# Small weights first in both load queues, all aggregation matmuls ahead of the first convolution, and one transpose for a unit's input where there were two

## The reference, cut to what matters

```python
# x (128, 64, 1024), cond (128, 128), all float32
x = x + conv1d(x, w0, pad=4, groups=4)            # w0 (64, 16, 9)
      + (cond @ cw.T)[:, :, None] + side[None, :, None]
h = gelu(cond @ W0 + b0);  h = gelu(h @ W1 + b1)
att = softmax(h @ W2 + b2)                        # (128, 8)
agg_w = einsum('bk,koi->boi', att, experts)       # one 64x64 matrix for each sample
x = x + einsum('boi,bih->boh', agg_w, x) + (att @ bias_k)[:, :, None]
```

## Time and profile before

| what | value |
|---|---|
| median of 3 runs | 252.88 us |
| the profiled execution | 252.83 us |
| its span, first to last instruction | 251.0 us |
| outside the span | 1.83 us |
| PE busy | 239.5 us, 95% |
| DVE busy | 223.1 us, 89% |
| ACT busy | 89.5 us, 36% |
| POOL busy | 27.1 us, 11% |
| moved by DMA | 68.72 MB, mean 274 GB/s |

### The profile page before, as it was taken

One profiled execution on the slowest core, in us unless ns is written; L12 is line 12 of the kernel. 1 busy time (PEld: TensorE's weight loads), 2 busy tenths in 40 slices (PEclk: granted clock), 3 DMA queues, 4 the chain that ended last, 5 costly groups with the idle time before them and its releaser, 6 DMA issues.

```text
span 251.0 us, 5804 instructions
## 1 busy us (share of the span) xinstructions
PE 239.5 (95%) x2180; PEld 95.4 (38%) x2180; DVE 223.1 (89%) x146; ACT 89.5 (36%) x144; POOL 27.1 (11%) x52
## 2 busy tenths in 40 slices
PE   7399999999999999999999999999999999999973
PEld 5263233333333333333333344344444444434531
DVE  0531899999999999999999999999999999999683
ACT  2305353321433333341505233333415052333453
POOL 1030422010101010010101010100101010101000
PEclk9659999999999999999999999999999999999999
DMA  6999693999999999999999999998989998444376
GB/s 145 262 306 274 136 200 60 334 231 407 329 375 240 381 240 339 293 319 305 272 350 238 387 228 373 276 361 249 335 292 287 342 262 347 167 167 168 123 293 256
DMA packets 29770, 68.72 MB, mean 274 GB/s; under 512 B 3312, under 2 KB 5616, under 8 KB 29760
## 3 DMA queue, kind: packets, MB, share of 16 engines
q1 hardware_dynamic: 19824, 51.41, 63.0%
q10 hardware_dynamic: 9936, 17.17, 26.2%
HBM read 35.02 MB, written 33.55 MB: 273 GB/s over the span
## 4 chain that ended last, share of the span: by engine, by line
PE 93%; DMA 2%; DVE 2%; SPq 1%; issue 0%; ACT 0%; DVEq 0%
PE yps L534 64%; PE zps L557 21%; DMA xin<-in_x 2%; PE yps L616 2%; PE yps L573 2%; PE zps L516 2%; DVE xph L414 1%; SPq L199 1%; DVE ynat L483 1%; PE zps L596 0%; PE yps L596 0%; PE zps L585 0%; PE zps L634 0%; DVE ycol L476 0%; ACT xin L380 0%
## 5 line engine op out<-in xcount | busy, mean ns | idle before, releaser
L534 PE MATMUL yps<-xph,wraw 64*64 64x512 f32 x1488 | 167.4, 591 | 0.0
L308 ACT ACTIVATE zout<-zps,gamu 128x512 f32<-128x512 f32 x120 | 72.9, 688 | 130.9 <-PE zps L557 87.9
L534 PEld LDWEIGHTS yps<-xph,wraw 64*64 64x64 f32 x1488 | 60.0, 132 | 100.2 <-issue 99.8
L422 DVE STREAM_TRANSPOSE ycol<-yps 128x1024 f32<-128x1024 f32 x62 | 74.5, 1220 | 9.2 <-PE yps L534 8.5
L414 DVE STREAM_TRANSPOSE xph<-xin 128x2112 f32<-128x2112 f32 x32 | 74.8, 2339 | 2.5 <-DMA xin<-in_x 2.5
L432 DVE STREAM_TRANSPOSE ynat<-ycol 128x2048 f32<-128x2048 f32 x30 | 67.6, 2291 | 1.1
L557 PE MATMUL zps<-ynat,mixv 64*64 64x512 f32 x480 | 57.6, 589 | 0.0
L244 POOL COPY mixv<-mixt 128x512 f32 (+1 forms) x16 | 17.5, 1094 | 178.9 <-ACT zout L308 174.5
L557 PEld LDWEIGHTS zps<-ynat,mixv 64*64 64x64 f32 x480 | 19.9, 132 | 30.3 <-issue 29.3
L316 ACT ACTIVATE mixt<-zps 128x1024 f32<-128x1024 f32 x8 | 7.8, 1021 | 17.3 <-PE zps L516 17.3
L616 PE MATMUL yps<-zout 128*128 128x256 f32 x20 | 8.9, 632 | 2.2 <-POOL zout L250 1.3
(11 more groups left out here) (54 smaller groups left out, 29.1 us busy)
## 6 DMA issues: line engine op xcount, KB each, us to landing
out<-zout SPq DMA_DIRECT2D x60, 512.0 KB, 5.3
xin<-in_x ACTq DMA_DIRECT2D x60, 258.0 KB, 7.5
xin<-in_x SPq DMA_DIRECT2D x60, 258.0 KB, 7.3
out<-xin SPq DMA_DIRECT2D x2, 512.0 KB, 3.2
out<-xin SPq DMA_DIRECT2D x4, 256.0 KB, 2.2
xin<-in_x ACTq DMA_DIRECT2D x4, 132.0 KB, 5.0
xin<-in_x SPq DMA_DIRECT2D x4, 130.0 KB, 5.0
xin<-in_x SPq DMA_DIRECT2D x4, 128.0 KB, 6.7
```

Of the source, the lines that this page charges most:

```text
L308: nc.scalar.activation(zout[:, o].rearrange("p (i c j q) -> p c i j q", i=2, c=2, q=PH)[:, c], zps[:, at:at + BANK].rearrange("p (q i j) - ...
L422: nc.vector.transpose(ycol[:, :, :, :, :, g].rearrange("p i s j q c -> p (i s j) q c"), yps[:, 2 * BANK * (g % 2):2 * BANK * (g % 2) + 2 * ...
L534: last = nc.tensor.matmul(yps[C * c:C * c + C, at:at + BANK].rearrange("p (s f) -> p s f", s=S // 2), wsum[rows, b, g], xph[slot][c][rows, ...
```

## The change

Seven edits are made together:

- SP issues `mlps`, `shares` and the experts `mixw` ahead of all of x; ACT issues `wraw` (the convolution weights) ahead of its part of x. `mixw` is 128 KB instead of 256 KB.
- `attt` is made by four ACT copies with a scale, where DVE made it in one instruction.
- The aggregation is two calls of 8 matmuls of 32 rows by 64 columns, where it was four calls of 4 matmuls of 32 rows by 128 columns; the even and odd channel blocks lie on the two partition halves of `mixt`. Four `gather` copies are left of eight.
- Both calls stand ahead of the first convolution, with `keep_on(3)` ahead of the transposed `att`, behind it, and between the calls; the `keep_on(6)` is gone.
- `mixv` is written by ACT in four copies of 64 partitions by 256 elements a unit, in the middle of the evacuation of the unit before, where POOL wrote it in one copy. POOL keeps `gamu`.
- A unit's x is turned in one transpose (4160 columns; unit 0 in two, of 2112 and 2048) and `ynat` is made in one (4096 columns).
- ACT's loads of unit 1 are issued in two halves, the second behind the `attt` copies; its load of unit 2 stands behind all gathers.

```diff
-        xph = [[sb(f"xph{i}{c}", [P, G, S // 2, NJ + 2, 2]) for c in range(2)] for i in range(2)]
+        xph = [sb(f"xph{i}", [P, G, S // 2, 2 * NJ + 2, 2]) for i in range(2)]
-        mixt = sb("mixt", [P, C, NS])
+        mixt = sb("mixt", [P, CH // 2, RT * RO, NS])
...
+        def mix_places(slot, h, d):
+            return mixv[slot][C * h:C * h + C].rearrange("p b (a d c) -> p d b a c", a=CH // 2, d=2)[:, d]
+        def mix_values(u, d):
+            return mixt[C * d:C * d + C, :, :, bass.ds(S * u, S)].rearrange("p a c b -> p b a c")
...
             sp.dma_start(mlps[:], mlp).then_inc(mlp_in, 16)
-            for k in range(KQ):
-                for t in range(2):
-                    sp.dma_start(*x_piece(0, 0, 0, k, t, 0)).then_inc(x_first, 16)
             sp.dma_start(shares[:], share).then_inc(share_in, 16)
-            for k in range(KQ):
-                for t in range(2):
-                    sp.dma_start(*x_piece(0, 0, 0, k, t, 1)).then_inc(x_in[0], 16)
-            sp.dma_start(wraw[:], conv_w).then_inc(w_in, 16)
+            sp.dma_start(mixw, mix_w).then_inc(mix_in, 16)
+            for part, there in ((0, x_first), (1, x_in[0])):
+                for k in range(KQ):
+                    for t in range(2):
+                        sp.dma_start(*x_piece(0, 0, 0, k, t, part)).then_inc(there, 16)
             sp.dma_start(consts, const_w).then_inc(const_in, 16)
...
+            def matrices(u, slot):
+                for h in range(2):
+                    for d in range(2):
+                        nc.scalar.activation(mix_places(slot, h, d), mix_values(u, d), ACT.Copy).then_inc(mixv_made, 1)
...
+            act.dma_start(wraw[:], conv_w).then_inc(w_in, 16)
             for k in range(KQ):
                 for t in range(2):
                     act.dma_start(*x_piece(0, 0, 1, k, t, 0)).then_inc(x_first, 16)
...
-            act.dma_start(mixw, mix_w).then_inc(mix_in, 16)
             act.wait_ge(beta_mm, 1)
             nc.scalar.activation(beta[0:C], gps[0:C, 0:NS], ACT.Identity, bias=fsides[0:C]).then_inc(beta_made, 1)
-            load(1, 1)
+            load_block(1, 1, 0)
+            act.wait_ge(share_in, 16)
+            act.wait_ge(mm, 4)
+            for o in range(RO):
+                nc.scalar.activation(attt[:, o], sps[:, 0:NS], ACT.Copy, scale=turn[:, o:o + 1]).then_inc(soft, 1)
+            load_block(1, 1, 1)
...
             with act.Fori(3, NU // 2) as i:
                 for c in range(2):
                     for o in range(PR):
                         evacuate(2 * i + c - 4, c, o)
                         if o == 1:
                             load(2 * i + c, c)
+                            matrices(2 * i + c - 3, 1 - c)
...
+            def turn_in(slot, at, to):
+                nc.vector.transpose(
+                    xph[slot][:, :, :, at:to].rearrange("q g s j t -> q j s g t"),
+                    xin[slot][:, :, PH * at:PH * to].rearrange("q c (j p) -> q j c p", p=PH)).then_inc(turned, 1)
+            def phases(u, slot):
+                dve.wait_ge(x_in[slot], 64 * u + 128 - 64 * slot)
+                if not (isinstance(u, int) and u < 2):
+                    dve.wait_ge(conv_done, 4 * u - 4)
+                turn_in(slot, 0, 2 * NJ + 2)
...
                 for g in range(G):
                     y_columns(u, g)
-                    if more and g < 2:
-                        phases(u + 1, 1 - slot, g)
-                for i in range(2):
-                    y_natural(u, slot, i)
+                    if more and g == 1:
+                        phases(u + 1, 1 - slot)
+                y_natural(u, slot)
...
             def aggregate(a):
                 for r in range(RT):
                     if a > 0 and r % 2 == 0:
                         pe.wait_ge(agg_out, 2 * a - 1 + r // 2)
-                    nc.tensor.matmul(zps[:, BANK * r:BANK * r + BANK], mixw[32 * r:32 * r + 32, a],
-                                     attt[32 * r:32 * r + 32].rearrange("p o b -> p (o b)"),
-                                     start=True, stop=True).then_inc(agg_mm, 1)
+                    for d in range(2):
+                        nc.tensor.matmul(zps[C * d:C * d + C, BANK * r:BANK * r + BANK],
+                                         mixw[32 * r:32 * r + 32, 2 * a + d],
+                                         attt[32 * r:32 * r + 32].rearrange("p o b -> p (o b)"),
+                                         start=True, stop=True).then_inc(agg_mm, 1)
...
-            pe.wait_ge(turned, 1)
-            keep_on(6)
+            keep_on(3)
+            first_aggregate()
+            keep_on(3)
+            second_aggregate()
             pe.wait_ge(w_in, 16)
-            conv(0, 0, 0, (first_aggregate,))
-            conv(0, 0, 1, (second_aggregate,))
-            conv(0, 0, 2, (output_constants, None, third_aggregate))
-            conv(0, 0, 3, (None, None, fourth_aggregate))
-            conv(1, 1, 0, (None, None, pair_constants))
+            pe.wait_ge(w_sum, 1)
+            conv(0, 0, 0)
+            conv(0, 0, 1, (output_constants,))
+            conv(0, 0, 2)
+            conv(0, 0, 3, (None, None, pair_constants))
+            conv(1, 1, 0)
```

More of the change, by code:

```diff
@@ L185, in load @@
                 if not (isinstance(u, int) and u < 2):
-                    sp.wait_ge(turned, 2 * u - 2)
+                    sp.wait_ge(turned, u)
                 for k in range(KQ):
@@ L237, in _, with constants_of @@
         def _(pool):
-            def matrices(u, slot):
+            def constants_of(u, slot):
                 if not (isinstance(u, int) and u < 2):
                     pool.wait_ge(z_made, 8 * u - 8)
[L242 to L245, removed]
                 if isinstance(u, int) and u == 0:
@@ L259, in _ @@
             for a in range(CH):
-                own = mixw[:, a].rearrange("p (d h g c) -> p d h g c", d=2, h=2, g=G)[:, :, :, a]
-                nc.gpsimd.tensor_tensor(own, own, same.rearrange("p (h c) -> p h c", h=2).unsqueeze(1)
-                                        .broadcast_to([P, 2, 2, 8]), ALU.add).then_inc(mix_eye, 1)
+                own = mixw[:, a].rearrange("p (h g c) -> p h g c", h=2, g=G)[:, :, a]
+                nc.gpsimd.tensor_tensor(own, own, same.rearrange("p (h c) -> p h c", h=2), ALU.add).then_inc(mix_eye, 1)
             pool.wait_ge(w_in, 16)
@@ L282, in _, with load_block @@
                                         ALU.mult, ALU.mult).then_inc(const_sum, 1)
-            matrices(0, 0)
-            matrices(1, 1)
+            constants_of(0, 0)
+            constants_of(1, 1)
             with pool.Fori(1, NU // 2) as i:
                 for c in range(2):
-                    matrices(2 * i + c, c)
+                    constants_of(2 * i + c, c)
         @block.scalar
         def _(act):
+            def load_block(u, slot, k):
+                for t in range(2):
+                    act.dma_start(*x_piece(slot, u, 1, k, t)).then_inc(x_in[slot], 16)
             def load(u, slot):
-                if not (isinstance(u, int) and u < 2):
-                    act.wait_ge(turned, 2 * u - 2)
+                act.wait_ge(turned, u)
                 for k in range(KQ):
-                    for t in range(2):
-                        act.dma_start(*x_piece(slot, u, 1, k, t)).then_inc(x_in[slot], 16)
+                    load_block(u, slot, k)
             def evacuate(u, slot, o):
@@ L356, in _ @@
                     load(3 + o // 2, 1 - o // 2)
+                if o == 1:
+                    matrices(1, 1)
             for o in range(PR):
@@ L369, in _ @@
                     evacuate(u, u % 2, o)
+                    if o == 1:
+                        matrices(u + 1, 1 - u % 2)
             act.wait_ge(gam_cut, NU)
-            act.wait_ge(turned, 2 * NU - 2)
+            act.wait_ge(turned, NU)
             def evacuate_first(o, c):
@@ L398, in _, with first_phases @@
         def _(dve):
[L399 to L416 removed]
+            def turn_in(slot, at, to):
+                nc.vector.transpose(
+                    xph[slot][:, :, :, at:to].rearrange("q g s j t -> q j s g t"),
+                    xin[slot][:, :, PH * at:PH * to].rearrange("q c (j p) -> q j c p", p=PH)).then_inc(turned, 1)
+            def first_phases(c):
+                if c == 0:
+                    dve.wait_ge(margins, 4)
+                    dve.wait_ge(x_first, 128)
+                    turn_in(0, 0, NJ + 2)
+                else:
+                    dve.wait_ge(x_in[0], 128)
+                    turn_in(0, NJ + 2, 2 * NJ + 2)
+            def phases(u, slot):
[3 more added lines that the diff above has]
+                turn_in(slot, 0, 2 * NJ + 2)
             def y_columns(u, g):
```

93 lines of the change are left out of this document (32 added, 61 removed).

## The result

The changed kernel takes 251.73 us (median of 5, 250.91 to 252.05) against 252.88 before: ratio 0.9948, 95% interval 0.9926 to 0.9969. It is faster, by 1.2 us where 3.7 was forecast, and 251.73 lies above the range of 247.4 to 251.1. The profiled execution took 251.88 us with a span of 250.1.

A forecast was written before the change was run, and what follows sets the result against it. PE (13.75 of 13.75 us) and DVE (13.68) were taken as full in a steady unit, so the gain lay in the head: 252.83 - 3.4 (head) - 0.2 (PE's waits for DVE) = 249.2 us, range 247.4 to 251.1.

The forecast's parts named there:

- T: End of the first two mixings in the head: 41.74 before, forecast 38.3, a gain of 3.4 us.
- s: Start of the first convolution on PE, forecast 18.0, 0.5 later than before; from it T would be s+19.6 = 37.6.
- L: Moment when all of unit 1's x has landed, forecast 22.5, bounds 21.5 to 24.5; from it T is L+15.8 = 38.3.
- the later of the two paths: Head: T follows the later of s+19.6 = 37.6 on PE and L+15.8 = 38.3 on DVE, so L's.
- PE's wait ahead of group 3: Head: PE waits about 1.2 us ahead of the fourth convolution group, until DVE's columns release it.
- rival 1: Head: clock stays at half up to the convolution; s 20 to 22, time 250.7 to 252.7; chance 0.12.
- (a): Condition for s: PE's own work ahead of the convolution ends at 17.95; 16.6 with the clock back at 11.7.
- (b): Condition for s: unit 0's second half landed at 14.9 and turned at 17.2, bounds 16.5 to 18.3.
- the bound of 2.14: Head: upper price of one aggregation call at full clock, if its narrow matmuls run four at a time; 1.07 was taken.
- Rivals 3 and 4: 3: DVE paces, larger gain, 246.4, chance 0.07. 4: merged transposes longer than two, gain lost, 252.6 to 253.5, chance 0.05.
- rival 2: Steady part: ACT's strided copies are dear, a two-unit loop of 24.0 + M in 27.5 decides from 3.5; 254.0; chance 0.06.
- M: Time of ACT's four mixv copies a unit: 1.8 forecast at 0.45 each, hidden under 2.8 of cover; 4.1 in rival 2.

The follow-up runs named there:

- e1: Changed kernel with ACT's four mixv copies of the steady part ahead of its four x loads, not behind them; 251.44 us, ratio 0.9938.
- e4: Changed kernel with the four mixv copies reading contiguous floats instead of every 128th one, so the matrices are not the samples' own; 250.23 us (one).
- e3: Changed kernel with the moves of e1 and e2 together; 249.82 us, ratio 0.9888.
- e5: e3 with unit 1's x turned in two transposes again, the second behind the second group's columns; 247.84 us, ratio 0.9801.
- e6: Kernel before with only the transposes merged, POOL still copying the matrices; 252.98 us, ratio 0.9995.
- e7: Changed kernel with each mixv copy writing its block twice (512 elements, second half unused), at the same place; 264.66 us, ratio 1.0463.
- e2: Changed kernel with only the last unit's copies moved, from the middle of unit 14's evacuation to the end of unit 13's; 251.05 us, ratio 0.9922.
- e10: e5 with the load order of the kernel before, aggregations still ahead of the convolution; 253.66 us, ratio 1.0030.
- e9: e5 with wraw issued on ACT behind all of unit 0's x instead of ahead of it; 248.95 us, ratio 0.9832.

## Why the prediction was right or wrong

**The head: right in size, with two terms that cancel.** T 38.40 against 38.3. The convolution started at 17.43 against s = 18.0, and unit 1's turning at 21.91 against L = 22.5, both within their bounds. So L was 0.6 early and the chain behind it 0.7 long, and that T came out 0.1 off is luck. From 21.91 the chain took 16.5 instead of the 15.8 of my sum: the gaps of 0.14 where PE waits for DVE, the start of the mixings (1.95 and not 1.72) and the convolution group (2.84). In all five profiles of this head (changed, e1 to e4) T comes 16.5 behind that transpose, so the later of the two paths set T as forecast. PE's wait ahead of group 3 was forecast 1.2, measured 1.09.

**Inside s.** The clock rose between 11 and 12 (0.64 in that stretch, 1.00 in the next), where I had 14.2 by carrying over the 6.0 us of the kernel before; so rival 1 (half clock up to the convolution) was wrong, and in the profiles of e3, e4 and e5 the clock stayed at 1.00 from 8 to the convolution, with 1.56 for three matmuls of zeros that take 2.75 at the half rate. PE's own work therefore ended at 16.8, near the 16.6 that I had given for an early rise, and what set s was not (a) but (b), unit 0's second half, turned at 17.17 (forecast 17.2). The eight narrow aggregation matmuls and the start of the convolution:

```profile
12.50 1.11 PE L533 MATMUL zps<-zout 32*64 32x512 f32 x16
17.43 3.67 PE L552 MATMUL yps<-xph,wraw 64*64 64x512 f32 x32 [0.62 <-DVE xph L418]
```

The taken 1.07 is right for the first call and the bound of 2.14 is out. The second call took 1.77, since its second half also waits for ACT to empty `zps`. By the Trainium skill's "TensorEngine Tiling (Array Packing)", section "Available Configurations", the 32 by 64 mode has eight tiles; eight matmuls side by side in the first line agree.

**DVE: right.** 4.47 and 4.42 were forecast, 4.473 and 4.445 measured. It had the room that was needed, and e6 shows that its saving is worth only the 0.2 in the steady part. Rivals 3 and 4 fall.

**ACT's copies: the step that failed.** The sentence was "Four take 1.8, hidden". Two sizes in it were off, the mechanism was rival 2's. A copy took 0.66 instead of 0.45, because I interpolated between contiguous rows and left the stride to the rival; M was 2.70. And the loop decides from 2.7 (24.8 worked out from e7), not from 3.5, since I had summed it without the gaps between engines. At 2.7 on 2.7 the loss was 1.21 us, where a gain of 0.2 was forecast. e1, e4 and e7 show it from three sides: the copies elsewhere, shorter, longer.

**The tail: priced at nothing, bound 1.8, measured 1.23.** Half of it is PE's wait ahead of the last unit (0.6), half the final stores (0.6), which I had not thought of. e2 gives back both. The 0.6 of the wait has a shown cause; that the stores lose theirs through unit 14's late ones is argued from their rows.

**The sum.** 249.2 + 1.4 (steady) + 1.2 (tail) + 0.1 (T) = 251.9; the profiled execution took 251.88. The range ended at 251.1 because I gave the copies no part in it: rival 2 was all or nothing in my chances, while its edge lay in the middle of my own bounds for M (1.4 to 4.1).

## What to carry to other kernels

Work moved to an engine that is idle half of the time is not free if it lands between two of its deadlines: look at the place, not the share, and put it where the engine waits for another. Close the loop through the engines and compare it with the period, gaps included; if price and cover are close, treat the result as open and let the range reach both ways. Price a copy by a row with its own stride, and when a step moves forward, move its loads forward with it: e10 shows that without them the step waits.

## What the runs showed that I had not expected

- The new head may make the time less steady. In one batch the kernel before spread over 1.2 us in 17 executions (252.40 to 253.63) and e1 over 3.3 in 11 (249.67 to 253.00); but in a later batch the kernel before spread over 2.2 in 13, and e5 over 0.65 in 5, so it isn't settled. With the same head T was 37.76 to 39.28 in five profiles, and each time the landing of x led: the chain there is DMA, where the kernel before waited behind PE's own matmuls.
- The recorded clock can stay at 1.00 when the work runs at the half rate. In e6 the twelve instructions of zeros took as long as in the earlier trace rows, where the record has 0.50; its timeline row:

```profile
12.00 5.49 PE L617 MATMUL yps<-zout 128*128 128x256 f32 x12 [0.63 <-DVE xph L401]
```

and one stretch of the same time, with 1.00 in the place of the clock (the number before 1.09):

```profile
14.00:15.00 1.00, 1.00 (x4) 0.82 (x3) 0.68 (x1) 0.00 (x0) 0.00 (x0) 1.00 1.09 231
```

The zeros of e9 and e10 above are two more cases. The duration of a known instruction is the surer sign.
- ACT's four load issues took from 2.85 to 3.34 us in the steady part of the changed kernel, in turn a longer and a shorter one. Five of the six mixings that waited stood behind issues of 3.10 to 3.34, and none behind the short ones of the loop (2.87 to 2.90). The sixth, at 64.17, stood behind one of 2.85, so the length of the issue isn't all that decides.
